# A two-layer graph network in one core: every engine's program reordered, and the row maxima of four heads turned, negated and placed together

## The chip, the cores and the metric

The kernel runs on 1 core of one Trainium2 chip, as one launch. The metric is device time in microseconds. The kernel before was run three times: 1134.08, 1138.78 and 1141.26 us, median 1138.78.

## The reference

16 graphs of 512 nodes with 256 features go through two layers. Everything is float32.

```python
# layer 0, 8 heads of 32, x: (16, 512, 256), adj: (16, 512, 512)
q, k, v = proj(Wq, bq), proj(Wk, bk), proj(Wv, bv)
scores = einsum('bhqd,bhkd->bhqk', q, k) / sqrt(32)
scores = where((adj + eye(n))[:, None] > 0, scores, -inf)
out = einsum('bhqk,bhkd->bhqd', softmax(scores), v) -> (b, n, 256)
h = x + out @ Wo.T + bo
x = (h - mean(h)) * rsqrt(var(h) + 1e-5) * gamma + beta
# layer 1, one head
f = x @ fc_w.T + fc_b
logits = (f @ q_w.T + q_b) + swap(f @ k_w.T + k_b)
masked = leaky_relu(logits + (1 - adj) * -1e9, 0.01)
return softmax(masked) @ f + x
```

## The kernel before, in words

Each engine has a program of its own, written out by hand: `iteration(t)` for t from -1 to 17, and in it 32 steps (`for s in range(POS)`). Iteration t does the attention of graph t, and beside it the first part (turned x, q, k, v, mask) of graph t + 1, the end of layer 0 and the start of layer 1 of graph t - 1, and the end of layer 1 of graph t - 2. `on(t, off)` says whether graph t + off exists. A piece's offset stands in the tables `PE_STEPS`, `ACT_STEPS`, `DVE_STEPS` and `POOL_STEPS`; PE's table also has the step. `Signal.after` turns a piece's name into a semaphore count, so the tables must have the order of the programs.

In every step TensorE (PE) makes one tile of transposed scores for four heads' group g, `st_bank` (a matmul of the stacked halves of q and k, L525, and one that adds the turned mask, L527), and one tile of scores the other way round, `sm_bank` (L535), from which VectorE (DVE) takes the row maxima (L947). ScalarE (ACT) makes the exponentials `e` of the first (L742). The maxima tiles run ahead of the exponentials by `LEAD` = 20 tiles: `maxima_tile(s)` gives tiles 0 to 11 of the next graph at steps 12 to 31, so that group 0 of the next graph begins at step 12 and group 1 at step 28. They read `q_pad`, q of a head among zeros, which four DMAs fill (`pad`, L286); PE waits for them before the first tile of a group.

The row maximum is put into the matmul as a 97th row of `q_stack`. For each head j of 8, PE turns a column of maxima (`turn_max`, L452, [4, 128] out), DVE negates it (`negate_max`, L874) into one of two slots of `neg_max`, and SyncE (SP) places it with a DMA (`place_max`, L291). A slot is written again only once the DMA of two heads before has landed. PE waits for `max_placed[i]` before the first tile of each head.

All DMAs are issued by SP, in one order (`iteration`, L293): adjacency in, `stack(1)` (24 DMAs, L277 and L278, from the halves of q and k into `q_stack` and `k_stack`), `pad(0)` (4), the adjacency again for layer 1, the outputs of graph t - 2, `stack(0)` (24), `pad(1)` (4), x for the residual into `h`, x of graph t + 2, and the eight maxima between them. The wait that opens the iteration on SP is for `l_max3`, DVE's last read of `adj_in` in layer 1.

Everything else on PE goes into three shared PSUM banks in turn (`FILLS`, `bank_of`): a piece waits until the piece three before it in the table has been read (`bank_read`). So the order in `PE_STEPS` also says which reader each piece waits for.

The pieces that the change moves: x turned (`turn_x`), q, k (`project_qk`) and v (`rows_times`); the products with v (`times_v`, L465, `o_bank`); the sums over keys (`total`, L475) of what GpSimd (POOL) added (`add_e`, L1044) and their reciprocals in quarters (DVE, L882); the output projection (`out_project`), residual, statistics and norm (L723); h turned (`turn_h`), `fc_project` and `key_logits`; layer 1's maxima (`layer1_maxima`, L929), leaky relu (`logits`, L677) and exponentials (L684); their turning (`turn_z`, L498) and the product with the features (`attend`, L509), added to h by `finish` (L893). POOL adds `bo` to the residual (L1104).

Of the kernel before, what the change touches and what calls it, by code (L numbers as in the profile page):

```python
# [23 lines left out]
F32R = mybir.dt.float32r  # L24
# [20 lines left out]
LEAD = 20  # L45
# [9 lines left out]
class Signal:  # L55
# [35 lines left out]
    **{f"m{j}": ("dve", f"m{j}") for j in range(NH)}}  # L91
ACT_STEPS = [
# [5 lines left out]
DVE_STEPS = [  # L98
# [5 lines left out]
POOL_STEPS = [  # L104
    ("sum1_3a", -1), ("sum1_3b", -1), ("o_norm0", -1), ("diag", 1), ("sum0_1a", 0), ("o_lo0", -1),
    ("o_norm1", -1), ("o_lo1", -1), ("sum0_1b", 0), ("sum0_2a", 0), ("sum0_2b", 0), ("l_mask", -1), ("sum0_3a", 0),
    ("sum0_3b", 0), ("neg_mean", -1), ("var_eps", -1), ("rstd", -1), ("shift", -1), ("h_gamma", -1), ("h_rest", -1),
    ("sum1_1a", 0), ("sum1_1b", 0), ("x_bo", 0), ("sum1_2a", 0), ("sum1_2b", 0)]
# [8 lines left out]
def build(nc, x, adj, wq, bq, wk, bk, wv, bv, wo, bo, gamma, beta, fc_w, fc_b, q_w, q_b, k_w, k_b, out):  # L117
    with ExitStack() as ctx:
# [47 lines left out]
        neg_max = sb("neg_max", [NT, 2, P], F32R)  # L166
# [55 lines left out]
        max_placed = [Signal(sem(f"max_placed{i}"), [("g1", 0), ("g0", 1)], 16) for i in range(GH)]  # L222
# [23 lines left out]
        def _(sp):  # L246
# [33 lines left out]
            def pad(g, t):  # L280

                sp.wait_ge(act_done.sem, act_done.after(f"q_hi{g}", t))
                sp.wait_ge(sm_done.sem, sm_done.after(27 if g == 0 else 11, t - 1 if g == 0 else t))
# [4 lines left out]
            def place_max(j, t):  # L288
                g, i = j // GH, j % GH
                sp.wait_ge(dve_done.sem, dve_done.after(f"m{j}", t))  # L290
                sp.dma_start(f(q_stack[g][STACK:STACK + 1, i, :]), f(neg_max[:, j % 2, :])).then_inc(max_placed[i].sem, 16)  # L291

            def iteration(t, par):  # L293
# [15 lines left out]
                if on(t, 0):  # L309
                    place_max(6, t)  # L310
                for half in range(2):
                    if on(t, -2):
                        sp.wait_ge(dve_done.sem, dve_done.after(f"fin{half}", t))
                        c = 2 * half
                        sp.dma_start(rows(out, t - 2, c, c + 2), h[par][:, c:c + 2, :]).then_inc(stored[half].sem, 16)
                if on(t, 0):
                    place_max(7, t)
                if on(t, 1):
# [3 lines left out]
                    place_max(0, t)  # L322
# [4 lines left out]
                if on(t, 1):  # L327
                    place_max(1, t)
                    place_max(2, t)
                if on(t, 2):  # L330
                    sp.wait_ge(pool_done.sem, pool_done.after("o_lo1", t))
                    sp.wait_ge(pe_done.sem, pe_done.after("xt1", t))
                    sp.dma_start(x_in[:, :, :], rows(x, t + 2)).then_inc(x_loaded.sem, 16)
                if on(t, 1):
                    place_max(3, t)
# [9 lines left out]
        def _(pe):  # L345
# [28 lines left out]
            def bank_read(name, t):  # L374
# [9 lines left out]
                return made[who].sem, made[who].after(reader, tb)  # L384
# [9 lines left out]
            def iteration(t, par):  # L394
# [52 lines left out]
                def turn_max(j):  # L447

                    pe.wait_ge(max_done.sem, max_done.after((4 * j + 15) % POS, t if j < 4 else t - (1 if 4 * j + 15 < POS else 0)))
                    pe.wait_ge(*bank_read(f"m{j}", t))  # L450
                    bank = bank_of[f"m{j}"]
                    nc.tensor.transpose(bank[0:NT, 0:P], row_max[:, j, :], ident[:, :]).then_inc(pe_done.sem, 1)  # L452
# [61 lines left out]
                for s in range(POS):  # L514
                    g, kt, i = s // (POS // 2), s // GH % NT, s % GH
                    if on(t, 0):
                        if kt == 0 and i == 0:
                            pe.wait_ge(stacked[g].sem, stacked[g].after(f"g{g}", t if g else t - 1))
                            if g == 0:
                                pe.wait_ge(act_done.sem, act_done.after("mt1", t - 1))  # L520
                        if kt == 0:
                            pe.wait_ge(max_placed[i].sem, max_placed[i].after(f"g{g}", t if g else t - 1))
# [14 lines left out]
                    if s == 0:  # L537
                        if on(t, 1):
                            turn_x(0)
                        if on(t, 0):  # L540
                            rows_times("v", 1, xt_hi, xt_lo, WV)
                    if s == 1:
                        if on(t, 1):
                            turn_x(1)
                    if s == 2:
                        if on(t, -1):
                            times_v(0)
                    if s == 3:
                        if on(t, -2):
                            turn_z(0)  # L550
                        if on(t, 0):
                            turn_max(4)
                    if s == 4:
                        if on(t, 1):
                            project_qk("q", WQ, 0)
                    if s == 5:
                        if on(t, -2):
                            turn_z(1)
                        if on(t, -1):
                            total(1)  # L560
                    if s == 6:
                        if on(t, 1):
                            project_qk("k", WK, 0)
                        if on(t, -2):
                            turn_z(2)
                    if s == 7:
                        if on(t, 0):
                            times_v(1)
                            turn_max(5)
                    if s == 8:  # L570
                        if on(t, -2):
                            turn_z(3)
                    if s == 9:
                        if on(t, 0):
                            turn_max(6)
                        if on(t, -2):
                            attend(0)
                    if s == 10:
                        if on(t, 0):
                            times_v(2)  # L580
                        if on(t, -2):
                            attend(1)
                    if s == 11:
                        if on(t, -2):
                            attend(2)
                    if s == 12:
                        if on(t, -2):
                            attend(3)
# [544 lines left out]
```

## Time and profile before

| what | value |
|---|---|
| runs | 1134.08, 1138.78, 1141.26 us |
| profiled execution: time, span | 1139.43 us, 1137.7 us |
| PE busy | 1039.8 us, 91% |
| DVE busy | 741.8 us, 65% |
| POOL busy | 723.9 us, 64% |
| ACT busy | 622.3 us, 55% |
| granted clock of PE, mean | 0.971 |
| chain that ended last | PE 62%, DVE 14%, ACT 11%, issue 6%, POOL 4% |

The busy time of an engine is the union of its instructions. Matmuls are pipelined, and a matmul's duration in the trace (586 ns for L535) is longer than the time after which the next can start, so PE's busy share says less than the distances between starts. The chain of waits shows those distances: it follows the last instruction back, at each step to what released it. The trace repeats from graph 2 on with a period of 65.0 us.

### The profile page before, as it was taken

What the parts mean: (1) busy time and instruction counts of PE and PEld (TensorE: products, weight loads), DVE (VectorE), ACT (ScalarE), POOL (GpSimd) and SP (SyncE); (2) the same over time, 40 slices, a digit from 0 to 9 for tenths busy, and PEclk for the clock granted to TensorE, in tenths of its full rate; (3) what the DMA queues carried; (4) which work ended last, traced back from release to release, by engine and by line L of the source; (5) the groups of instructions that cost most, each with busy time, mean ns of one, the idle gap of its engine ahead of it and who ended that gap; (6) DMA issues with size and microseconds to landing.
All of it is one profiled execution on the core that took longest, in us unless ns stands there. A gap on an engine that the chain in (4) does not pass through costs nothing.

```text
span 1137.7 us, 17894 instructions
## 1 busy us (share of the span) xinstructions
PE 1039.8 (91%) x5896; PEld 653.8 (57%) x5896; DVE 741.8 (65%) x1959; ACT 622.3 (55%) x1178; POOL 723.9 (64%) x415
## 2 busy tenths in 40 slices
PE   4788899999999999999999999999999999999676
PEld 3444455656666565666656565666656566665354
DVE  4554767676766768676766767676676867675332
ACT  2144466574737556564746657473755656474623
POOL 3054686676776666686766667677666668677840
PEclk9798999999999999999999999999999999999967
DMA  5344545353434445353444534353444435334010
GB/s 139 84 103 103 140 103 140 81 134 99 132 101 100 137 104 124 99 135 99 127 113 103 140 83 132 100 133 99 101 137 104 120 102 135 100 80 114 1 56 18
DMA packets 90763, 121.01 MB, mean 106 GB/s; under 512 B 18480, under 2 KB 45616, under 8 KB 90672
## 3 DMA queue, kind: packets, MB, share of 16 engines
q1 hardware_dynamic: 90672, 119.87, 40.4%
q8 instruction: 48, 0.79, 0.3%
q14 instruction: 43, 0.35, 0.1%
HBM read 52.44 MB, written 8.39 MB: 53 GB/s over the span
## 4 chain that ended last, share of the span: by engine, by line
PE 62%; DVE 14%; ACT 11%; issue 6%; POOL 4%; SPq 2%; DMA 1%; ACTq 0%; DVEq 0%; POOLq 0%
PE shared L391 16%; PE shared L509 10%; PE st_bank L525 8%; PE st_bank L527 7%; PE o_bank L465 7%; PE sm_bank L535 7%; DVE recip L882 3%; ACT z L677 3%; DVE sm_bank L947 3%; ACT e L742 3%; POOL e_sum L1044 2%; DVE masks L937 2%; PE shared L498 2%; DVE qt_lo L865 2%; PE shared L484 2%
## 5 line engine op out<-in xcount | busy, mean ns | idle before, releaser
L742 ACT ACTIVATE e<-st_bank 128x512 f32<-128x512 f32 x512 | 309.1, 605 | 396.5 <-PE st_bank L527 394.2
L947 DVE CUSTOM_DVE_ANT_0 sm_bank<-sm_bank,masks 128x512 f32<-128x512 f32 x512 | 351.7, 695 | 239.3 <-PE sm_bank L535 237.4
L535 PE MATMUL sm_bank<-kt_hi,q_pad 128*128 128x512 f32 x512 | 299.0, 586 | 17.0 <-issue 6.0
L1044 POOL TENSOR_TENSOR e_sum<-e_sum,e 128x1024 f32<-128x1024 f32 x128 | 302.2, 2390 | 6.2 <-ACT e L742 5.0
L525 PE MATMUL st_bank<-q_stack,k_stack 97*128 97x512 f32 x512 | 237.1, 464 | 0.8 <-ACT e L742 0.8
L527 PE MATMUL st_bank<-mask_t,ident_b 128*128 128x512 bf16 x512 | 201.7, 394 | 0.0
L1044 POOL TENSOR_TENSOR e_sum<-e 128x1024 f32<-128x1024 f32 x64 | 152.1, 2387 | 10.6 <-PE shared L475 8.2
L525 PEld LDWEIGHTS st_bank<-q_stack,k_stack 97*128 97x128 f32 x512 | 97.4, 190 | 93.6 <-issue 53.7
L465 PE MATMUL o_bank<-e,v 128*32 128x512 f32 x1024 | 137.2, 608 | 1.3 <-ACT e L742 1.3
L509 PE MATMUL shared<-feat,z 128*128 128x256 f32 x512 | 128.3, 397 | 1.4 <-ACT z L689 1.4
L535 PEld LDWEIGHTS sm_bank<-kt_hi,q_pad 128*128 128x128 f32 x512 | 104.7, 205 | 23.2 <-issue 11.9
L509 PEld LDWEIGHTS shared<-feat,z 128*128 128x128 f32 x512 | 98.5, 197 | 31.6 <-issue 11.7
L1096 POOL TENSOR_TENSOR h<-h,gamma_row 128x1024 f32<-128x1024 f32 x16 | 38.3, 2396 | 118.0 <-PE shared L484 118.0
L527 PEld LDWEIGHTS st_bank<-mask_t,ident_b 128*128 128x128 bf16 x512 | 50.1, 98 | 98.7 <-issue 85.5
L391 PE MATMUL shared<-weight_hi,split_hi 128*128 128x256 f32 x256 | 74.6, 292 | 1.5 <-DVE split_lo L861 1.5
L391 PE MATMUL shared<-weight_lo,split_hi 128*128 128x256 f32 x256 | 72.2, 282 | 0.0
L391 PE MATMUL shared<-weight_hi,split_lo 128*128 128x256 f32 x256 | 72.1, 282 | 0.0
L391 PE MATMUL shared<-xt_hi,weight_hi 128*128 128x512 f32 x128 | 52.8, 412 | 20.3 <-DVE qt_lo L865 18.4
L947 DVE DVE_READ_ACCUMULATOR2_ANT row_max<- 128x1 f32 x512 | 71.2, 139 | 0.0
L874 DVE TENSOR_SCALAR neg_max<-shared 4x128 fp32r<-4x128 f32 x128 | 35.0, 274 | 52.1 <-DMA q_stack<-neg_max 47.9
L1049 POOL TENSOR_TENSOR x_in<-x_in 128x512 f32<-128x512 f32 x16 | 20.4, 1274 | 65.0 <-DVE x_in L882 63.3
L882 DVE RECIPROCAL x_in<-x_in 128x128 f32<-128x128 f32 x64 | 55.7, 907 | 9.1 <-ACT x_in L689 9.1
(126 smaller groups left out, 1830.8 us busy)
## 6 DMA issues: line engine op xcount, KB each, us to landing
adj_in<-in_adj SPq DMA_DIRECT2D x32, 1024.0 KB, 5.8
q_stack<-qt_hi SPq DMA_DIRECT2D x256, 64.0 KB, 2.0
k_stack<-kt_hi SPq DMA_DIRECT2D x256, 64.0 KB, 2.0
x_in<-in_x SPq DMA_DIRECT2D x16, 512.0 KB, 4.4
q_pad<-qt_hi SPq DMA_DIRECT2D x128, 64.0 KB, 2.0
q_stack<-qt_lo SPq DMA_DIRECT2D x128, 64.0 KB, 2.0
k_stack<-kt_lo SPq DMA_DIRECT2D x128, 64.0 KB, 2.0
h<-in_x SPq DMA_DIRECT2D x16, 512.0 KB, 3.8
```

What stands on the lines that cost most here:

```text
L391: last = nc.tensor.matmul(bank, a, b, start=(kt == 0 and n == 0), stop=(kt == kts - 1 and n == 2))
L465: last = nc.tensor.matmul(o_bank[i * DH:(i + 1) * DH, :], v[:, kt, o:o + DH], e[:, kt, i, :], start=(kt == 0), stop=(kt == NT - 1))
L509: last = nc.tensor.matmul(bank[:, k * D:(k + 1) * D], z[:, c, kt * P:(kt + 1) * P], feat[:, kt, :], start=(kt == 0), stop=(kt == NT - 1))
L525: nc.tensor.matmul(bank[:, :], k_stack[g][:, i, kt * P:(kt + 1) * P], q_stack[g][:, i, :], start=True, stop=False)
L527: nc.tensor.matmul(bank[:, :], ident_b[:, :], mask_t[par][:, kt, :], start=False, stop=True).then_inc(st_done.sem, 1)
L535: nc.tensor.matmul(sm_bank[s % 2][:, :], q_pad[j // GH][:, j % GH, qt * P:(qt + 1) * P], kt_hi[j // GH][:, :], start=True, stop=True).then ...
L742: nc.scalar.activation(e[:, kt, i, :], st_bank[s % 2][:, :], ACT.Exp, scale=SCALE)\
L874: nc.vector.tensor_scalar(neg_max[:, j % 2, :], bank_of[f"m{j}"][0:NT, 0:P], -1.0, None, ALU.mult)\
L882: last = nc.vector.reciprocal(recip[g][:, n], recip[g][:, n])
L947: nc.vector.tensor_tensor_reduce(sm_bank[s % 2][:, :], sm_bank[s % 2][:, :], mask[nxt if off else par][:, qt * N:(qt + 1) * N], 1.0, LOWES ...
L1044: nc.gpsimd.tensor_tensor(e_sum[:, pair, :], a, b, ALU.add).then_inc(pool_done.sem, 1)
L1096: nc.gpsimd.tensor_tensor(hh[:, :, :], hh[:, :, :], every_row(gamma_row), ALU.mult).then_inc(pool_done.sem, 1)
```

## The change

The eight turned, negated and placed maxima become two, one for each group of four heads: `turn_max(g)` turns [128, 16] at once, `neg_max` has a slot of 16 rows for each group, and one DMA places the 16 rows as 2048 elements of row 97. PE waits for it once, at the first tile of a group. `LEAD` becomes 21, so the groups of the next graph begin at steps 11 and 27. Nearly every other piece has another step. The work itself, apart from the six turns, negations and DMAs fewer, is the same.

```diff
-LEAD = 20
+LEAD = 21
 PE_STEPS = [
-    (0, "xt0", 1), (0, "v1", 0), (1, "xt1", 1), (2, "pv0", -1), (3, "et0", -2), (3, "m4", 0), (4, "q0", 1),
-    (5, "et1", -2), (5, "sum1", -1), (6, "k0", 1), (6, "et2", -2), (7, "pv1", 0), (7, "m5", 0), (8, "et3", -2),
-    (9, "m6", 0), (10, "pv2", 0), (10, "at0", -2), (12, "at1", -2), (13, "op0", -1), (14, "m7", 0),
-    (14, "pv3", 0), (15, "op1", -1), (16, "q1", 1), (17, "mt0", 1), (18, "k1", 1), (18, "m0", 1), (18, "pv4", 0),
-    (21, "sum0", 0), (22, "m1", 1), (22, "pv5", 0), (22, "ht0", -1), (23, "ht1", -1),
-    (25, "mt1", 1), (25, "m2", 1), (26, "pv6", 0), (26, "fc0", -1), (27, "fc1", -1), (28, "kb", -1),
-    (29, "v0", 1), (30, "m3", 1), (30, "pv7", 0)]
+    (0, "pv0", -1), (1, "xt0", 1), (1, "xt1", 1), (4, "sum1", -1), (5, "q0", 1),
+    (6, "k0", 1), (8, "pv1", 0), (8, "et0", -2), (9, "et1", -2), (10, "pv2", 0),
+    (11, "at0", -2), (12, "m1", 0), (12, "et2", -2), (13, "pv3", 0), (14, "et3", -2), (14, "q1", 1),
+    (15, "op0", -1), (16, "op1", -1), (17, "k1", 1), (18, "pv4", 0), (19, "mt0", 1), (20, "sum0", 0), (21, "mt1", 1),
+    (21, "pv5", 0), (22, "ht0", -1), (23, "ht1", -1), (23, "at1", -2), (25, "pv6", 0),
+    (26, "fc0", -1), (27, "fc1", -1), (28, "v0", 1), (28, "m0", 1), (29, "kb", -1), (30, "pv7", 0), (31, "v1", 1)]
 DVE_STEPS = [
...
+    ("x_lo0", 1), ("x_lo1", 1), ("mask", 1), ("q_lo0", 1), ("k_lo0", 1), 
+    ("recip1", -1), ("l_recip", -2), ("m1", 0), ("fin0", -2), ("q_lo1", 1),
+    ("h_add0", -1), ("stats_a", -1), ("h_add1", -1), ("stats_b", -1), ("moments", -1), ("k_lo1", 1), 
+    ("h_lo0", -1), ("h_lo1", -1), ("recip0", 0), ("fin1", -2), ("q_dot0", -1), ("q_dot1", -1), ("m0", 1), ("l_max1", -1),
+    ("l_max3", -1)]
 POOL_STEPS = [
...
+    ("sum1_3a", -1), ("sum1_3b", -1), ("x_bo", -1), ("o_norm0", -1), ("diag", 1), ("sum0_1a", 0), ("o_lo0", -1),
+    ("sum0_1b", 0), ("sum0_2a", 0), ("sum0_2b", 0), ("o_norm1", -1), ("l_mask", -1), ("o_lo1", -1), ("sum0_3a", 0),
+    ("sum0_3b", 0), ("neg_mean", -1), ("var_eps", -1), ("rstd", -1), ("shift", -1), ("sum1_1a", 0), ("sum1_1b", 0),
+    ("h_gamma", -1), ("h_rest", -1), ("sum1_2a", 0), ("sum1_2b", 0)]
-        neg_max = sb("neg_max", [NT, 2, P], F32R)
+        neg_max = sb("neg_max", [GH * NT, NG, P], F32R)
-        max_placed = [Signal(sem(f"max_placed{i}"), [("g1", 0), ("g0", 1)], 16) for i in range(GH)]
+        max_placed = [Signal(sem(f"max_placed{g}"), [("max", 1 - g)], 16) for g in range(NG)]
             # SP
+            def place_max(g, t):
+                sp.wait_ge(dve_done.sem, dve_done.after(f"m{g}", t))
+                sp.dma_start(f(q_stack[g][STACK:STACK + 1, :, :]), f(neg_max[:, g, :])).then_inc(max_placed[g].sem, 16)
             def iteration(t, par):
...
                     stack(1, t)
-                    place_max(4, t)
                 if on(t, 1):
                     pad(0, t)
-                if on(t, 0):
-                    place_max(5, t)
                 if on(t, -1):
...
                     sp.dma_start(adj_in[:, :, :], rows(adj, t - 1)).then_inc(adj_loaded.sem, 16)
+                if on(t, -2):
+                    store(0, t, par)
                 if on(t, 0):
-                    place_max(6, t)
...
+                    place_max(1, t)
                 if on(t, 1):
                     sp.wait_ge(st_done.sem, st_done.after(POS // 2 - 1, t))
                     stack(0, t)
                     pad(1, t)
-                    place_max(0, t)
+                if on(t, 2):
...
+                    sp.dma_start(x_in[:, :, :], rows(x, t + 2)).then_inc(x_loaded.sem, 16)
+                if on(t, -2):
+                    store(1, t, par)
                 if on(t, 0):
...
                     sp.dma_start(h[par][:, :, :], rows(x, t)).then_inc(h_loaded.sem, 16)
                 if on(t, 1):
...
+                    place_max(0, t)
             # PE
-                def turn_max(j):
+                def turn_max(g):
+                    last = (g * GH * NT + GH * NT - 1 - LEAD) % POS
+                    pe.wait_ge(max_done.sem, max_done.after(last, t))
+                    pe.wait_ge(*bank_read(f"m{g}", t))
+                    nc.tensor.transpose(bank_of[f"m{g}"][0:GH * NT, 0:P],
+                                        row_max[:, g * GH:(g + 1) * GH, :].rearrange("p h q -> p (h q)"), ident[:, :])\
+                        .then_inc(pe_done.sem, 1)
                 def attend(c):
...
-                    if c == 0:
-                        pe.wait_ge(act_done.sem, act_done.after("et3", t))
+                    pe.wait_ge(act_done.sem, act_done.after(f"et{c}", t))
             # ACT: logits 2, 3 at steps 0, 1 of the next iteration; exponentials 0 to 3 at steps 4, 6, 8, 10
             # (before: 0, 1, 3, 4); turned_z at 9, 10, 13, 15; turned_mask at 20, 22; o_high(1) at 13
             # DVE: mask halves at steps 4, 5; reciprocals(1) at 8 to 11, reciprocals(0) at 21 to 24;
             # finish at 13 and 25; layer1_maxima at 30 and 31; negate_max(1) at 12, negate_max(0) at 29
```

(The last four lines tell the moved steps of ACT and DVE in words.)

## Rows read from the trace of the kernel before

**Rows 1.** Windows: stretch, its us, busy us of each engine (instructions), PE clock, DMA

```profile
54.52:171.06 116.54, 104.32 (x560) 58.22 (x558) 73.89 (x197) 57.96 (x101) 68.69 (x36) 0.94 0.44 109
171.06:1016.63 845.57, 814.46 (x4759) 513.91 (x4758) 594.67 (x1574) 497.96 (x950) 581.13 (x326) 1.00 0.43 114
1016.63:1137.70 121.07, 90.55 (x457) 59.79 (x455) 46.76 (x120) 54.44 (x110) 64.71 (x39) 0.84 0.17 48
431.25:496.32 65.07, 62.66 (x368) 39.54 (x366) 45.69 (x122) 38.32 (x74) 44.29 (x26) 1.00 0.44 114
...
459.37:496.32 36.95, 36.80 (x226) 23.36 (x224) 24.95 (x76) 20.21 (x36) 27.29 (x16) 1.00 0.37 94
```

**Rows 2.** Chain of waits in the iteration from 431.25: start us, us, what

```profile
457.32 0.24 PE st_bank L525
457.56 0.23 PE st_bank L527
457.79 0.23 PE sm_bank L535
458.02 1.73 PE shared L509 x8
...
462.88 1.40 PE shared L391 x12
...
464.98 0.11 PE shared L452
465.08 1.00 PE o_bank L465 x8
466.08 0.43 PE st_bank L525
...
481.78 0.44 PE shared L484 x4
```

**Rows 3.** Waits over the whole run: engine, line, releaser: total us, times, longest

```profile
PE shared L391 <- DVE qt_lo L865: 18.4, 16, 1.7
...
PE sm_bank L535 <- DMA q_pad<-qt_hi: 4.4, 1, 4.4
```

**Rows 4.** Timeline of DVE: the last instruction of `layer1_maxima`

```profile
431.29 0.08 DVE L929 DVE_READ_ACCUMULATOR2_ANT z<- 128x1 f32 x1
```

**Rows 5.** Timeline of SP's queue from 432.37: first and last of 24 stacks

```profile
432.37 0.59 SPq L291 DMA_DIRECT2D q_stack<-neg_max  x1
433.00 0.44 SPq L296 DMA_DIRECT2D adj_in<-in_adj  x1
433.54 0.56 SPq L277 DMA_DIRECT2D q_stack<-qt_hi  x1
...
448.58 0.59 SPq L278 DMA_DIRECT2D k_stack<-kt_lo  x1
...
449.94 2.42 SPq L286 DMA_DIRECT2D q_pad<-qt_hi  x4
```

**Rows 6.** The tile q_pad, from 431 to 497: its DMAs

```profile
DMA to landing us min/median/max: 1.9/2.0/2.0
```

**Rows 7.** Timeline of PE at step 12 of graph 0

```profile
73.45 0.39 PE L527 MATMUL st_bank<-mask_t,ident_b 128*128 128x512 bf16 x1
77.09 0.47 PE L535 MATMUL sm_bank<-kt_hi,q_pad 128*128 128x512 f32 x1 [3.26 <-issue]
```

**Rows 8.** Windows around that wait, columns as in rows 1

```profile
73.80:77.10 3.30, 0.04 (x2) 0.04 (x1) 0.65 (x3) 0.60 (x1) 2.34 (x1) 1.00 0.35 80
...
78.80:82.20 3.40, 3.40 (x13) 0.89 (x12) 1.08 (x4) 0.56 (x1) 2.30 (x1) 0.50 0.02 5
```

**Rows 9.** Groups by line: shapes, count | busy us, mean ns | idle before, releasers

```profile
L1104 POOL TENSOR_TENSOR h<-h,bo_row 128x1024 f32<-128x1024 f32 x16 | 38.3, 2395 | 10.1 <-DMA h<-in_x 9.6
L723 ACT ACTIVATE h<-h,shift,rstd 128x256 f32<-128x256 f32 x64 | 35.1, 607 | 13.9 <-POOL shift L1092 13.9
L874 DVE TENSOR_SCALAR neg_max<-shared 4x128 fp32r<-4x128 f32 x128 | 35.0, 274 | 52.1 <-DMA q_stack<-neg_max 47.9 <-PE shared L391 3.7 <-PE shared L452 0.4
```

More of the change, by code:

```diff
@@ L282, in pad @@
                 sp.wait_ge(act_done.sem, act_done.after(f"q_hi{g}", t))
-                sp.wait_ge(sm_done.sem, sm_done.after(27 if g == 0 else 11, t - 1 if g == 0 else t))
+                sp.wait_ge(sm_done.sem, sm_done.after((GH * NT - 1 - LEAD) % POS if g == 0 else (POS - 1 - LEAD) % POS, t - 1 if g == 0 else t))
                 for i in range(GH):
@@ L286, in pad, with store @@
                     sp.dma_start(f(q_pad[g][r, i, :]), f(qt_hi[g][r, :])).then_inc(padded[g].sem, 16)
[L288 to L291, printed above, removed]
+            def place_max(g, t):
+                sp.wait_ge(dve_done.sem, dve_done.after(f"m{g}", t))
+                sp.dma_start(f(q_stack[g][STACK:STACK + 1, :, :]), f(neg_max[:, g, :])).then_inc(max_placed[g].sem, 16)
+            def store(half, t, par):
+                sp.wait_ge(dve_done.sem, dve_done.after(f"fin{half}", t))
+                c = 2 * half
+                sp.dma_start(rows(out, t - 2, c, c + 2), h[par][:, c:c + 2, :]).then_inc(stored[half].sem, 16)
             def iteration(t, par):
@@ L383, in bank_read @@
                 who, reader = READ_BY[other]
-                return made[who].sem, made[who].after(reader, tb)
+                later = OFF[other] - made[who].offs[made[who].place[reader]]
+                return made[who].sem, made[who].after(reader, tb + later)
             def three_terms(bank, terms, kts=DT):
@@ L548, in iteration @@
-                    if s == 3:
+                    if s == 0 and on(t, -1):
+                        times_v(0)
+                    if s == 1 and on(t, 1):
+                        turn_x(0)
+                        turn_x(1)
+                    if s == 4 and on(t, -1):
+                        total(1)
+                    if s == 5 and on(t, 1):
+                        project_qk("q", WQ, 0)
+                    if s == 6 and on(t, 1):
+                        project_qk("k", WK, 0)
+                    if s == 8:
+                        if on(t, 0):
+                            times_v(1)
@@ L566, in iteration @@
[L566 to L582, printed above, removed]
@@ L599, in iteration @@
-                    if s == 16:
+                    if s == 10 and on(t, 0):
+                        times_v(2)
+                    if s in (11, 12) and on(t, -2):
+                        attend(s - 11)
+                    if s == 12 and on(t, 0):
+                        turn_max(1)
+                    if s in (12, 14) and on(t, -2):
+                        turn_z(2 if s == 12 else 3)
+                    if s == 13 and on(t, 0):
+                        times_v(3)
+                    if s == 14:
@@ L609, in iteration @@
                         if on(t, 0):
                             times_v(4)
+                    if s == 19 and on(t, 1):
+                        turn_mask(0)
+                    if s == 20 and on(t, 0):
+                        total(0)
                     if s == 21:
-                        if on(t, 0):
-                            total(0)
-                    if s == 22:
                         if on(t, 1):
-                            turn_max(1)
+                            turn_mask(1)
@@ L696, in values @@
                     act.wait_ge(pe_done.sem, pe_done.after("pv6" if half == 0 else "pv0", t))
-                    copy(v[:, 2 * half:2 * half + 2, :], f"v{half}",
-                         bank_of[f"v{half}"][:, :].rearrange("p (k n) -> p k n", k=2))
+                    act.wait_ge(pe_done.sem, pe_done.after(f"v{half}", t if half == 0 else t - 1))
+                    nc.scalar.copy(v[:, 2 * half:2 * half + 2, :], bank_of[f"v{half}"][:, :].rearrange("p (k n) -> p k n", k=2))\
+                        .then_inc(act_done.sem, 1)
                 def turned_mask(half):
@@ L744, in iteration @@
                     if s == 0 and on(t, -2):
-                        exponentials(0)
-                    if s in (1, 2) and on(t, 1):
-                        if s == 1:
-                            act.wait_ge(pe_done.sem, pe_done.after("v1", t))
-                        copy(xt_hi[:, s - 1, :], f"xt{s - 1}", bank_of[f"xt{s - 1}"][:, :])
-                    if s == 1 and on(t, -2):
-                        exponentials(1)
-                    if s == 2 and on(t, 0):
-                        values(1)
@@ L754, in iteration @@
-                    if s == 3 and on(t, -2):
-                        exponentials(2)
-                    if s == 4 and on(t, -2):
-                        turned_z(0)
-                    if s == 4 and on(t, -1):
+                        logits(2)
+                    if s == 1 and on(t, 0):
+                        values(1)
+                    if s == 1 and on(t, -2):
+                        logits(3)
+                        act.wait_ge(act_done.sem, act_done.after("logit3", t))
+                        nc.scalar.mul(l_negmax[:, :], z[:, :, N], -1.0).then_inc(act_done.sem, 1)
@@ L759, in iteration @@
+                    if s == 2 and on(t, 1):
+                        act.wait_ge(pe_done.sem, pe_done.after("v1", t - 1))
+                        copy(xt_hi[:, 0, :], "xt0", bank_of["xt0"][:, :])
+                        copy(xt_hi[:, 1, :], "xt1", bank_of["xt1"][:, :])
+                    if s == 3 and on(t, -1):
                         copy(o_raw[1][:, :], "pv0", o_bank[:, :])
                     if s == 4 and on(t, -2):
-                        exponentials(3)
-                    if s == 5 and on(t, 1):
+                        exponentials(0)
@@ L763, in iteration @@
+                    if s == 5 and on(t, -1):
+                        copy(recip[1][:, :], "sum1", bank_of["sum1"][:, :])
+                    if s == 6 and on(t, 1):
                         qk_high("q", qt_hi, 0, 0)
                     if s == 6 and on(t, -2):
-                        turned_z(1)
-                    if s == 6 and on(t, -1):
-                        copy(recip[1][:, :], "sum1", bank_of["sum1"][:, :])
+                        exponentials(1)
+                    if s == 7 and on(t, 1):
+                        qk_high("k", kt_hi, 1, 0)
@@ L768, in iteration @@
                     if s == 7 and on(t, -1):
                         o_high(0)
-                    if s == 7 and on(t, 1):
-                        qk_high("k", kt_hi, 1, 0)
-                    if s == 7 and on(t, -2):
+                    if s == 8 and on(t, -2):
+                        exponentials(2)
+                    if s == 9 and on(t, -2):
+                        turned_z(0)
+                    if s == 10 and on(t, -2):
+                        turned_z(1)
+                        exponentials(3)
@@ L866, in qk_lo, with negate_max @@
                                                    f(hi[g][:, :]), ALU.add, ALU.subtract).then_inc(done, 1)
[L868 to L874 removed]
+                def negate_max(g):
+                    dve.wait_ge(pe_done.sem, pe_done.after(f"m{g}", t))
+                    dve.wait_ge(max_placed[g].sem, max_placed[g].after("max", t - 1))
+                    nc.vector.tensor_scalar(neg_max[:, g, :], bank_of[f"m{g}"][0:GH * NT, 0:P], -1.0, None, ALU.mult)\
                         .then_inc(done, 1)
@@ L878, in reciprocals @@
                     if quarters[0] == 0:
-                        dve.wait_ge(act_done.sem, act_done.after(f"sum{g}", t if g else t - 1))
+                        dve.wait_ge(act_done.sem, act_done.after(f"sum{g}", t))
                     for k in quarters:
@@ L931, in layer1_maxima, with make_mask @@
                     last.then_inc(done, 1)
-                def make_mask():
-                    dve.wait_ge(adj_loaded.sem, adj_loaded.after("adj", t))
-                    for c in range(2):
-                        to = slice(c * 2 * N, (c + 1) * 2 * N)
-                        last = nc.vector.tensor_scalar(mask[nxt][:, to], adj_in[:, 2 * c:2 * c + 2, :].rearrange("p c n -> p (c n)"),
-                                                       0.0, -BIG, ALU.is_le, ALU.mult)
-                    last.then_inc(done, 1)
+                def make_mask(c):
+                    if c == 0:
+                        dve.wait_ge(adj_loaded.sem, adj_loaded.after("adj", t))
+                    to = slice(c * 2 * N, (c + 1) * 2 * N)
+                    last = nc.vector.tensor_scalar(mask[nxt][:, to], adj_in[:, 2 * c:2 * c + 2, :].rearrange("p c n -> p (c n)"),
+                                                   0.0, -BIG, ALU.is_le, ALU.mult)
+                    if c == 1:
+                        last.then_inc(done, 1)
                 for s in range(POS):
@@ L970, in iteration @@
                         nc.vector.reciprocal(l_recip[:, :], l_sum[:, :]).then_inc(done, 1)
+                    if s in (8, 9, 10, 11) and on(t, -1):
+                        reciprocals(1, (s - 8,))
+                    if s == 12 and on(t, 0):
+                        negate_max(1)
+                    if s == 13 and on(t, -2):
                         dve.wait_ge(pool_done.sem, pool_done.after("h_rest", t - 1))
                         finish(0)
-                    if s == 13 and on(t, -2):
-                        finish(1)
-                    if s == 14 and on(t, -1):
-                        add_residual(0)
-                    if s == 15 and on(t, 0):
-                        negate_max(7)
-                    if s == 15 and on(t, -1):
-                        statistics(0)
-                    if s == 16 and on(t, -1):
-                        add_residual(1)
-                        statistics(1)
+                    if s == 15 and on(t, 1):
+                        qk_lo("q", 1, 0, qt_lo, qt_hi)
+                    if s in (16, 17) and on(t, -1):
+                        add_residual(s - 16)
+                        statistics(s - 16)
+                    if s == 18 and on(t, 1):
+                        qk_lo("k", 1, 1, kt_lo, kt_hi)
                     if s == 17 and on(t, -1):
@@ L1061, in iteration @@
                     add_e(1, 3, 1)
+                    pool.wait_ge(h_loaded.sem, h_loaded.after("x_again", t - 1))
+                    hh = h[nxt]
+                    nc.gpsimd.tensor_tensor(hh[:, :, :], hh[:, :, :], every_row(bo_row), ALU.add).then_inc(pool_done.sem, 1)
                 if on(t, -1):
```

214 lines of the change are left out of this document (59 added, 155 removed), and 15 rows, old and new, of tables (ACT_STEPS, DVE_STEPS).

## The prediction, made before the changed kernel was run

> **What bounds the kernel now.** I read the windows first. From graph 2 to graph 14 the run is 13 equal periods, 845.57 us together, 65.04 each; ahead lie graphs 0 and 1 (116.54 us), behind are graph 15 and the tail (121.07 us) [rows 1]. PE is busy 62.66 us of one period, but that overstates it, since a matmul's record outlasts the distance to the next. So I priced PE by the chain of waits [rows 2]: 0.24 + 0.23 + 0.23 = 0.70 us for a bare step, 1.40 for a projection of 12 passes (q and k have 6 wider ones, the same 1.40), 1.73 for an `attend`, 1.00 for a product with v and another 0.20 because the score matmul behind it takes 0.43 and not 0.23, the same 1.20 for a `total`, 0.44 for four turned blocks, 0.11 for a turned maximum. A period adds up to: 32 steps 22.4; 8 products and 2 totals 12.0; 2 q and 2 k 5.6; v, output and features, two each, and the key logits 9.8; 4 `attend` 6.9; ten groups of turns (two of them masks, taken at the same 0.44) 4.4; 8 maxima 0.9. That is **62.0 us of work in 65.04**; 3.0 us is waiting. The second half has none to speak of: PE is busy 36.80 of the last 36.95 us, steps 12 to 31 [rows 1]. The waiting is in the first twelve steps, which take 65.07 - 36.95 = 28.1 us, and its largest part is q's projection group waiting for DVE: 18.4 us over 16 graphs on PE alone [rows 3].
>
> **Part 1: six turned maxima fewer.** PE saves 6 x 0.11 = 0.66 us a period [rows 2]. DVE saves 6 x 0.27 = 1.6 us, and the 47.9 us in which it stood before `neg_max` for the DMA of two heads earlier [rows 9], 3.0 a period; DVE isn't the bound on average (45.69 of 65.07 [rows 1]), so this pays only through the waits of the first steps. SP saves six issues of 0.63. The negation of 16 rows I take as that of 4, since its free length is the same 128. No row has the landing of the one larger DMA; I take the 2.0 us of the pads [rows 6], with 0 and 4 as ends.
>
> **Part 2: the first steps, unloaded.** Reciprocals of group 0, `attend` and half of layer 1's activations leave steps 0 to 10 or spread over them. Work up to the first maxima tile of the next graph, which is now at step 11: eleven bare steps and 0.47 are 8.2; `times_v` three times, `total` once 4.8; x turned 0.9; q and k 2.8; two z turned 0.9. Together 17.5 us from the iteration's start; before, step 12 came after 28.1. If nothing else waits, a period is 62.0 - 0.66 = 61.4 us.
>
> **Part 3: SP's queue is now late.** This is where I expect the gain to stop. That tile reads `q_pad`, and `pad(0)` stands on SP behind the adjacency load and 24 stacks. Now: last read of `adj_in` ends at 431.37 [rows 4], 0.1 us after the iteration's start; adjacency at 433.00, first stack at 433.54, the pads at 449.94, a maximum between [rows 5]. The distance from first stack to pads without that maximum (0.72) is 15.7. After the change the adjacency load waits for `layer1_maxima` at steps 30 and 31, one step later and behind one more row maximum on DVE (0.61 to 0.7): I estimate its end at 1.0 us after the start (0.1 to 1.3). Then 0.54 to the first stack, 15.7 to the pads, three issues of 0.62, and 2.0 to land [rows 6]: **21.1 us**. PE is there at 17.5. It stands 3.6 us. Before, the pads landed at 18.7 + 1.85 + 2.0 = 22.6 us after the start and PE came at 28.6, so the same queue cost nothing. The trace has this very wait once: at graph 0, where layer 1 has no work and PE ran ahead, it stood from 73.84 to 77.09 [rows 7], 4.4 us by the waits' own account [rows 3].
>
> From that tile to the next start: before, from step 12, 36.95 - 0.46 = 36.5 us. Now added: a step 0.70, three more `attend` 5.19, two turned z 0.88, half of v 1.40; less three maxima 0.33: 44.3. I take off 0.9 for small waits there that go (bounds 0.4 and 1.4), and add 0.6: ACT now does a mask copy and a sum copy among the four norm activations (607 ns each [rows 9]), so the turning of h comes later. **44.0 us**, and the period is 21.1 + 44.0 = 65.1, between 64.1 and 66.2. The loop closes through SP, so a faster or slower first half changes nothing.
>
> **Part 4: the clock.** At graph 0 the 3.26 us of standing came at full clock, and from 78.8 to 82.2 the granted clock was 0.50, which is 1.2 GHz, while PE was busy all 3.40 us [rows 8]. That did 1.7 us of work in 3.4. Where the slow stretch starts within the wait, less is lost. I take 1.2 us a period, ends 0 and 1.7. The Trainium skill (TensorE: Matmul & The Clock Gate, "HAM oscillation") says that a loop in which PE waits for a DMA in every turn pays for the lower clock in every turn. By the row alone the price is certain once, 1.7 us in the run; by the rule it comes 13 times, and the sum is some 15 us higher. The row agrees with the rule for one wait, and none in this trace shows it repeated.
>
> **Part 5: the ends.** Graph 0's wait of rows 7 ends about 2 us earlier, as SP starts the stacks at once; half of v (1.4) moves ahead of graph 0; graph 1 has no `attend` and is held by the same pads, about 54 us. I sum graphs 0 and 1 to 7 us less (3 to 10). In the tail `bo` is added behind the last sum of exponentials and no longer ahead, 2.4 us [rows 9], the adjacency mask (on POOL) comes ahead of the last low half, and `attend` overlaps more: 3 us less (0 to 6).
>
> **The sum.** 13 x (65.1 + 1.2 - 65.04) = +16; -7 - 3: +6 on the profiled execution's own 1139.4 is 1145. That execution lies 0.65 us above the median of 1138.8, so I say **1144 us**. What I cost at nothing: diagonal, statistics and turned masks, which keep their work and sit beside PE's 44 us; if PE didn't have them as cover they'd cost DVE's and ACT's time, at most 1 us a period.
>
> **The rivals.**
> - *The pads aren't what PE waits for* (the queue is ahead by a reason that I miss, or PE's part before is covered). Period 61.4: 13 x -3.6 = -47, with the ends -57: **1082**. For it: the work sum. Against: 24 issues at 0.63 are the steadiest thing in the trace. 12%.
> - *The pads land, but some 2 us earlier* than I have it, or the second half sheds more waits: period 64 without a slow clock, -13 - 10: **1116**. 10%.
> - *As forecast, but the clock stays at 1.00*: 1130. For it: the many short waits of the steady state never lowered it (1.00 over 845.57 us [rows 1]); against it: rows 8. 25%.
> - *The forecast*, 38%.
> - *Slower: the maxima of group 1 come late.* `place_max(1)` is queued on SP behind `store(0)`, which waits for `finish(0)` of step 13. By my count step 13's maximum ends 1.7 us after the step's start, `finish` 0.9 later, the store takes 1.2 of SP, then an issue and 2.0 to land: 5.9. PE needs it at step 16, 6.3 after. Before, each head's own placement lay apart from the others. If it lands more than 0.4 us later, PE stands there, and `max_placed` now holds all four heads. With 1.5 us a period on top of the forecast: **1164**. Only a page has something on the DMA's own cost: the Trainium skill (DMA: Bandwidth & Descriptors, "Anatomy of one DMA") gives about 2.0 us fixed for another issuing path, by which the sum would stay as it is. 15%.
>
> **How the numbers follow.** Two kernels within 1% (1127.4 to 1150.2) are about what can't be told from no change. Faster: all of the first two rivals and a third of the third, 30%. Slower: the last, and the upper part of the forecast's spread (clock 1.7, 44.9 us behind the pads: 1160), 24%. The rest, 46%, within. The range leaves out the first rival and half of the last: 1110 to 1160.
>
> **What would show it.** PE standing 2.5 to 4.5 us in every period just ahead of an `sm_bank` matmul of step 11, released by the DMA into `q_pad`, and no wait for `qt_lo` in steps 5 and 6. Granted clock under 1.00 in the steady state; 0.97 there means a slow stretch in most periods. If the wait is under 1 us, or PE comes to step 11 later than 20 us after the start, part 2 is wrong. If the period is under 63, part 3 is. If PE waits ahead of step 16's `st_bank`, the last rival holds.

## The result, and the profile after

The changed kernel takes **1148.56 us** (median of 4 runs, 1145.00 to 1151.18), the kernel before 1139.69 beside it (4 runs): ratio 1.0081, 95% interval 1.0057 to 1.0105. So 0.8% slower, where 1144 had been forecast.

The windows of the changed kernel, cut at the starts of graphs 0, 2 and 15 as in [rows 1], and two single periods. Columns as there: busy us of PE, PE's weight loads, DVE, ACT, POOL, then PE's clock.

```profile
55.96:166.71 110.75, 100.10 (x546) 55.80 (x547) 74.67 (x185) 57.30 (x102) 71.95 (x38) 0.97 0.45 115
166.71:1032.79 866.08, 824.61 (x4682) 522.55 (x4681) 592.85 (x1496) 501.10 (x950) 580.66 (x326) 0.97 0.42 111
1032.79:1143.20 110.41, 81.92 (x442) 53.74 (x440) 42.42 (x110) 53.87 (x109) 61.08 (x37) 0.94 0.18 52
569.50:633.98 64.48, 61.93 (x362) 39.20 (x361) 45.61 (x116) 38.54 (x74) 44.67 (x26) 1.00 0.43 115
302.13:370.29 68.16, 64.77 (x362) 41.10 (x361) 45.59 (x116) 38.54 (x74) 44.66 (x26) 0.95 0.41 109
```

The 13 periods take 866.08 us, 66.62 each and not 65.04: 20.5 us lost. The ends give back 16: graphs 0 and 1 took 116.54 and take 110.75, graph 15 and the tail took 121.07 and take 110.41. Ahead of graph 0, which starts at 55.96 and not 54.52, 1.4 more are lost. Of two periods one lasts 64.48 us at full clock, less than any of before, the other 68.16 at 0.95. The profiled execution is the fastest of the four, 1145.00 us.

The waits of PE on other things, the counterpart of [rows 3]. The wait for `qt_lo` is no longer among them. Sixteen waits ahead of the maxima tile, `sm_bank`, stand first; 13 of them, 40.3 us, are one in each period, 2.5 to 4.0 us long.

```profile
PE sm_bank L529 <- issue: 47.9, 16, 4.0
...
PE sm_bank L529 <- DMA q_pad<-qt_hi: 5.6, 2, 3.4
```

Three timelines of the period at full clock from 569.50: the last of layer 1's maxima on DVE, SP's adjacency, first and last stack and pads, and PE at step 11.

```profile
570.11 0.08 DVE L881 DVE_READ_ACCUMULATOR2_ANT z<- 128x1 f32 x1
```

```profile
570.22 0.37 SPq L300 DMA_DIRECT2D adj_in<-in_adj  x1
570.69 0.51 SPq L276 DMA_DIRECT2D q_stack<-qt_hi  x1
...
585.18 0.59 SPq L277 DMA_DIRECT2D k_stack<-kt_lo  x1
585.87 2.43 SPq L285 DMA_DIRECT2D q_pad<-qt_hi  x4
588.40 0.53 SPq L309 DMA_DIRECT2D adj_in<-in_adj  x1
```

```profile
586.61 0.49 PE L519 MATMUL st_bank<-q_stack,k_stack 97*128 97x512 f32 x1
586.95 0.39 PE L521 MATMUL st_bank<-mask_t,ident_b 128*128 128x512 bf16 x1
589.81 0.47 PE L529 MATMUL sm_bank<-kt_hi,q_pad 128*128 128x512 f32 x1 [2.48 <-issue]
```

Step 11 starts 17.1 us after the start of the period, and its two score matmuls take PE to about 17.7. The four pads go out from 16.4 to 18.2 and land 2.0 later, at 20.2, and the tile starts at 20.3. The trace names "issue" as what ended the wait, since it doesn't tie these landings to the matmul; the landing is 0.1 us ahead of it in every period. From the tile to the next start it is 44.2 us, in which PE is busy all the time:

```profile
589.80:633.98 44.18, 44.12 (x265) 30.03 (x266) 30.92 (x81) 22.24 (x40) 29.80 (x18) 1.00 0.37 102
```

In the longer period the same wait, 3.32 us, ends in a stretch at 0.50, the lower level of 1.2 GHz. It began 0.9 us before the wait ended, and PE works through the rest of it:

```profile
323.29 0.76 PE L529 MATMUL sm_bank<-kt_hi,q_pad 128*128 128x512 f32 x1 [3.32 <-issue]
```

```profile
323.40:326.80 3.40, 3.40 (x8) 2.71 (x9) 1.56 (x3) 0.00 (x0) 1.50 (x2) 0.50 0.84 288
323.30:370.29 46.99, 46.94 (x265) 31.90 (x266) 30.90 (x81) 22.24 (x40) 28.91 (x18) 0.94 0.36 95
```

From this tile to the next start it is 47.0 us and not 44.2. The 13 periods fall into three kinds. Four are at full clock, 44.1 to 44.2 us behind the tile; five have one stretch of 3.4 us at the lower level, 45.5 to 45.9 behind it; four have 6.8 us of it, 46.7 to 47.0 behind it. Added up, the lower level costs 19 us behind the tiles. The length of the wait alone doesn't decide which kind a period is: behind a wait of 2.49 us the clock was at the lower level (66.14 us, clock 0.97), and behind one of 3.15 it was not (65.13 us, clock 1.00).

```profile
721.81 0.76 PE L529 MATMUL sm_bank<-kt_hi,q_pad 128*128 128x512 f32 x1 [2.49 <-issue]
853.23 0.47 PE L529 MATMUL sm_bank<-kt_hi,q_pad 128*128 128x512 f32 x1 [3.15 <-issue]
```

### The profile page after: what moved, and what is told of

Read it like the earlier page. It is cut to its first block and busy times, and to the rows that moved or that the text cites. A ratio compares the mean times of both kernels' runs of the same rounds, so it can differ in the third digit from the quotient of the medians.

```text
span 1143.2 us, 17238 instructions
## 1 busy us (share of the span) xinstructions
PE 1039.5 (91%) x5800; PEld 656.8 (57%) x5800; DVE 737.4 (65%) x1863; ACT 624.2 (55%) x1178; POOL 723.1 (63%) x415
## 5 line engine op out<-in xcount | busy, mean ns | idle before, releaser
L529 PE MATMUL sm_bank<-kt_hi,q_pad 128*128 128x512 f32 x512 | 299.5, 587 | 57.1 <-issue 47.9
L504 PE MATMUL shared<-feat,z 128*128 128x256 f32 x512 | 137.9, 419 | 2.1 <-ACT z L640 2.1
L504 PEld LDWEIGHTS shared<-feat,z 128*128 128x128 f32 x512 | 108.6, 215 | 20.3 <-ACT z L640 2.7
L1006 POOL TENSOR_SCALAR_AFFINE_SELECT masks<-masks 128x512 bf16<-128x512 bf16 x16 | 10.3, 641 | 121.5 <-DVE masks L889 121.5
L834 DVE RECIPROCAL recip<-recip 128x128 f32<-128x128 f32 x64 | 60.5, 946 | 12.8 <-ACT recip L640 12.7
L834 DVE RECIPROCAL x_in<-x_in 128x128 f32<-128x128 f32 x64 | 60.1, 944 | 4.5 <-ACT x_in L640 4.5
L386 PEld LDWEIGHTS shared<-weight_hi,split_hi 128*128 128x128 f32 x256 | 48.2, 188 | 7.6 <-POOL split_lo L990 5.9
```

The costliest lines, as they stand in the source:

```text
L386: last = nc.tensor.matmul(bank, a, b, start=(kt == 0 and n == 0), stop=(kt == kts - 1 and n == 2))
L504: last = nc.tensor.matmul(bank[:, k * D:(k + 1) * D], z[:, c, kt * P:(kt + 1) * P], feat[:, kt, :], start=(kt == 0), stop=(kt == NT - 1))
L529: nc.tensor.matmul(sm_bank[s % 2][:, :], q_pad[j // GH][:, j % GH, qt * P:(qt + 1) * P], kt_hi[j // GH][:, :], start=True, stop=True).then ...
L834: last = nc.vector.reciprocal(recip[g][:, n], recip[g][:, n])
L1006: nc.gpsimd.affine_select(out=mask_diag[nxt], in_=mask_diag[nxt], compare_op=ALU.not_equal, fill=0.0, base=0, pattern=[[0, NT], [-1, P]], ...
```

## The experiments

The theory: SP's queue of 24 stacks ahead of the pads holds each period from its front, and the wait lets the clock fall behind it. The times below come with the kernel before on the same chip: 1140.19 us in the first four, 1139.10 in the last four.

### 1. The pads earlier

```diff
-                    stack(1, t)
+                    stack(1, t, (0, 1))
                 if on(t, 1):
                     pad(0, t)
+                if on(t, 0):
+                    stack(1, t, (2, 3))
```

> The changed kernel, with the four DMAs into q_pad of group 0 moved on SP between the 12 stacks of two heads and the 12 of the other two. Theory (the pads behind 24 stacks hold the period): they land about 14.6 us after the start of a period, PE comes to the tile of step 11 at 17.1 and doesn't wait there; the next thing late is layer 1's adjacency, still behind all stacks: it lands near 26.7, its mask and the last low half end near 30, and PE stands some 2 to 3 us ahead of the output projection of step 15. Period about 64.5 us, time 1110 to 1130. Rival (the tile waits for something else, such as DVE's row maxima): the wait ahead of step 11 stays and the time is that of the changed kernel, 1148.

Measured: 1125.69 us, ratio 0.9877 (0.9841 to 0.9913). The tile of step 11 no longer waits. PE waits instead ahead of the output projection, for the low half that POOL makes once the adjacency is there. PE's waits, and POOL in the period from 295.77:

```profile
PE shared L388 <- POOL split_lo L992: 42.4, 16, 7.6
```

```profile
317.62 1.27 POOL L988 TENSOR_TENSOR x_in<-x_in 128x512 f32<-128x512 f32 x1
322.50 1.90 POOL L1021 TENSOR_SCALAR adj_in<-adj_in 128x2048 f32<-128x2048 f32 x1 [3.61 <-DMA adj_in<-in_adj]
324.48 1.26 POOL L992 TENSOR_TENSOR split_lo<-x_in,split_hi 128x512 fp32r<-128x512 f32 x1
```

The low half ends at 325.7, 30.0 us after the start, as expected. PE's projection follows at 325.80, behind a gap of 2.15 us. The 13 periods average 65.5 and not 64.5. This wait, 1.8 to 3.4 us in a period, goes with the lower level too: it comes at or just behind the wait in seven periods, and the six at full clock last 63.8 to 64.9. The profiled execution is the slowest of the four, 1131.19 us. Its 13 periods:

```profile
166.35:1018.47 852.12, 818.68 (x4598) 520.22 (x4681) 594.68 (x1496) 501.06 (x950) 579.71 (x326) 0.98 0.42 113
```

### 2. Pads and second adjacency earlier

The same, and `stack(1, t, (2, 3))` stands behind the second adjacency load.

> As the run before, and the second adjacency load also ahead of the last 12 stacks. Theory: neither the tile of step 11 nor the projection of step 15 waits, the period is PE's work, 61.5 to 62.5 us, the clock stays at 1.00, time 1060 to 1085. Rival (the second half hides other waits, which come out once the first is gone, such as the stacks of group 1, now 3 us later, ahead of step 16): period 64 and more, time over 1110.

Measured: **1077.21 us**, ratio 0.9450 (0.9424 to 0.9475); 6% below the changed kernel. SP's order in the period from 468.94, and the windows of all 13 periods:

```profile
477.03 0.60 SPq L277 DMA_DIRECT2D k_stack<-kt_lo  x1
479.93 2.41 SPq L285 DMA_DIRECT2D q_pad<-qt_hi  x4
482.43 0.53 SPq L309 DMA_DIRECT2D adj_in<-in_adj  x1
483.00 1.58 SPq L276 DMA_DIRECT2D q_stack<-qt_hi  x1
```

```profile
160.24:963.60 803.36, 801.92 (x4598) 509.63 (x4681) 593.39 (x1496) 501.07 (x950) 580.39 (x326) 1.00 0.45 120
```

61.80 us a period at full clock, PE busy 801.92 of 803.36. The prediction's sum of PE's work was 61.4. The second half hid nothing large.

### 3. One tile less of lead

```diff
-LEAD = 21
+LEAD = 20
```

> The changed kernel with LEAD = 20 as before, so that the first tile that reads q_pad is at step 12 and not 11; nothing else differs. Theory: the pads land at 21.1 to 21.3 us as now, but PE has 2.4 us more to do ahead of them and comes at 19.6 to 20; it stands 1 to 1.5 us and not 3.5, the clock stays at 1.00, the period is 62 to 62.5 us, time 1080 to 1095. Rival (the stall is not the pads): same time as the changed kernel, 1148, or slower by the tile less ahead.

Measured: 1092.26 us, ratio 0.9582 (0.9557 to 0.9607). One number is worth 56 us. The pads land as before (20.2 to 21.3), and PE has `attend(0)` and a step ahead of them, 2.4 us. The wait is left at 0.1 to 1.1 us, and the clock holds. PE at step 12 of the period from 415.02, and the windows:

```profile
434.87 0.39 PE L521 MATMUL st_bank<-mask_t,ident_b 128*128 128x512 bf16 x1
435.84 0.47 PE L529 MATMUL sm_bank<-kt_hi,q_pad 128*128 128x512 f32 x1 [0.58 <-issue]
```

```profile
164.09:979.22 815.13, 805.38 (x4597) 509.46 (x4681) 592.18 (x1496) 501.11 (x950) 580.23 (x326) 1.00 0.44 118
```

### 4. Work inside the wait

```diff
                             pe.wait_ge(act_done.sem, act_done.after(f"k_hi{j // GH}", t))
+                            if j == 0:
+                                pe.wait_ge(max_done.sem, max_done.after((s - 2) % POS, t if s >= 2 else t - 1))
+                                for _ in range(12):
+                                    nc.tensor.matmul(sm_bank[s % 2][:, :], weight_hi[:, WQ, 0, 0:P],
+                                                     weight_hi[:, WQ, :, :].rearrange("p a b -> p (a b)"), start=True, stop=True)
                             pe.wait_ge(padded...)
```

> The changed kernel, with 12 matmuls of constant weights (512 columns each, into the bank that the tile then overwrites) put ahead of PE's wait for the pads, 2.8 us of work inside a wait of 3.5 us. Their results are not used. Theory of the clock: periods keep the 64.5 us that the changed kernel's periods have when its clock doesn't fall, against 66.6 on average; granted clock 1.00 between 100 and 1030 us, time 1115 to 1130. Rival (the differences between periods have another cause than the clock): the time stays at 1148 or more.

Measured: 1123.43 us, ratio 0.9845 (0.9815 to 0.9876). More work makes the changed kernel 25 us faster. The pads come no earlier, but PE spends the wait working, and no stretch between graph 2 and graph 15 is at the lower level:

```profile
376.94 3.12 PE L530 MATMUL sm_bank<-weight_hi 128*128 128x512 f32 x12
379.89 0.39 PE L534 MATMUL sm_bank<-kt_hi,q_pad 128*128 128x512 f32 x1
```

```profile
165.82:1010.67 844.85, 839.68 (x4748) 537.96 (x4837) 593.23 (x1496) 501.13 (x950) 581.46 (x326) 1.00 0.43 114
```

The first six of these periods last 64.5 to 64.7 us, the others 64.9 to 65.7, as the last of the pads then went out up to 1.2 us later. So the clock's price is 866.08 - 844.85 = 21 us of 13 periods; the 19 us counted in the changed kernel's own trace agree. The late queue itself costs 844.85 - 803.36 = 41 us. That is pads and second adjacency together: with the pads alone early (run 1) the 13 periods give back only 14 us. The second adjacency alone early was not tried.

### 5. The merged maxima alone

The kernel before, with `turn_max(g)`, `negate_max(g)`, `place_max(g)` and `max_placed` of the change at steps 12 and 28:

```diff
-    ... (3, "m4", 0) ... (7, "m5", 0) ... (9, "m6", 0) ... (14, "m7", 0) ... (18, "m0", 1) ... (30, "m3", 1) ...
+    ... (12, "m1", 0), (12, "at1", -2) ... (28, "m0", 1), (28, "kb", -1) ...
```

> The kernel before with one part of the change: the maxima of four heads turned, negated and placed as one, at steps 12 and 28, LEAD 20 and every other piece where it was. Theory: PE saves 0.66 us of turns a period, and the waits of the first steps lose DVE's stops before neg_max (3.0 us a period of DVE, of which PE feels less than 1): period 63.5 to 64.4, time 1118 to 1131. Rival (the turns and negations lie in waits of the first steps and pay nothing): 1135 to 1141. Rival (the one DMA now holds four heads and comes late ahead of step 16 or of the next start): slower than 1145.

Measured: 1121.20 us, ratio 0.9846 (0.9830 to 0.9863). This part of the change is good by itself. How is less plain than expected. The 13 periods give only 3.2 us; the rest comes from the ends: 2.2 ahead of graph 0, 7.9 in graphs 0 and 1 (108.7 us and not 116.5), 5.9 behind. Five periods last 63.9, as expected, eight 65.3 to 65.4. In every period PE waits ahead of k's projection in step 6 until DVE has read q's out of the same bank (`qt_lo`). Before, that wait was 1.1 us and never went with a slower clock. Now PE comes there 0.8 us sooner, since the wait of 0.6 us for `neg_max` ahead of `total` is gone, DVE is no sooner, and the wait is 2.0. It is the same 2.0 us in all thirteen periods, and in eight of them the clock falls:

```profile
PE shared L380 <- DVE qt_lo L846: 31.1, 16, 2.2
```

The wait before, and with the merged maxima:

```profile
445.17 0.47 PE L391 MATMUL shared<-xt_hi,weight_hi 128*128 128x512 f32 x1 [1.12 <-DVE qt_lo L865]
```

```profile
433.54 0.47 PE L380 MATMUL shared<-xt_hi,weight_hi 128*128 128x512 f32 x1 [2.00 <-DVE qt_lo L846]
```

```profile
290.31:355.66 65.35, 63.36 (x356) 40.13 (x360) 45.23 (x116) 38.12 (x74) 44.67 (x26) 0.97 0.42 114
355.66:419.52 63.86, 61.86 (x354) 38.99 (x360) 45.23 (x116) 38.12 (x74) 44.72 (x26) 1.00 0.42 116
```

### 6. The control: pads earlier in the kernel before

The edit of run 1 in the kernel before, its placements of maxima 4 and 5 behind the two halves of the stacks.

> The kernel before, its pads moved between the 12 stacks of two heads and the 12 of the others, as in the run that helped the changed kernel. Theory (before, the pads landed 6 us ahead of need, so SP's queue cost nothing): no difference, 1136 to 1143. Rival (SP's order costs both kernels): faster by more than 1%.

Measured: 1131.71 us, ratio 0.9938 (0.9918 to 0.9959): under the 1136 to 1143 expected and less than the rival's 1%, a miss, by a place that [rows 7] already show. The periods are the same, 845.44 us for 845.57. In graphs 0 and 1 the wait of 3.26 us is gone, and of 14.0 us at the lower level 3.4 are left; together that is 6 us. Another 3.4 us come off the tail (117.6 for 121.1), whose order was not touched; its clock was 0.88 and not 0.84.

```profile
54.34:164.83 110.49, 100.11 (x549) 56.51 (x558) 73.94 (x197) 58.12 (x102) 68.72 (x36) 0.98 0.45 115
164.83:1010.27 845.44, 814.72 (x4677) 514.02 (x4758) 595.30 (x1574) 497.07 (x950) 581.11 (x326) 1.00 0.42 114
```

### 7. Six turns put back

```diff
+                        if s in (3, 7, 10, 18, 22, 26):
+                            nc.tensor.transpose(sm_bank[s % 2][0:NT, 0:P], ident[:, 0:NT], ident[:, :])
```

> The changed kernel with pads and second adjacency early, and six turns of 4 columns of the identity more in a period, each into the bank that the maxima tile behind it overwrites; their results are not used. It gives back PE's part of what merging took away, without negations and DMAs. Theory: where PE is the bound, each costs its 0.11 us: period 61.7 + 0.66 = 62.4, time 1083 to 1089 against 1077. Rival (PE has room between its matmuls): 1077.

Measured: 1085.22 us, ratio 0.9525 (0.9506 to 0.9543), against 1077.21 for run 2 and 1076.62 for run 8, which was on the same chip. The periods take 810.10 and not 803.36 us: 6.7 by 78 turns, 0.09 each.

```profile
159.34:969.44 810.10, 809.08 (x4676) 514.51 (x4759) 593.92 (x1496) 501.13 (x950) 580.02 (x326) 1.00 0.45 119
```

### 8. Both edits

Run 2 with `LEAD = 20`.

> The changed kernel with pads and second adjacency early and LEAD = 20. Theory: with the pads in time the lead of a tile decides nothing, PE's work is the bound: period 61.7 us, time 1074 to 1081. Rival (a lead of 21 is worth something once the stall is gone): slower than 1082.

Measured: 1076.62 us, ratio 0.9452 (0.9436 to 0.9468). The same as run 2: once the pads are in time, the lead decides nothing.

## Why the prediction was right

**Part 1** had PE's price right: 0.11 us a turn said, 0.09 measured where PE is the bound (run 7). As records in the trace the turn of 16 columns takes 280 ns for 275, the negation of 16 rows 276 ns for 274 [rows 9], and DVE's 47.9 us of waiting before `neg_max` for a DMA are gone. The larger DMA landed after 1.9 us, 3.6 at most; 2.0 had been taken.

**Part 2**, PE at the tile of step 11 after 17.5 us: it comes at about 17.7. The waits of the first steps are gone. The largest of them had been read as q's projection; it stood ahead of k's (run 5), which changes no number here.

**Part 3** is the one that decided. First stack at 1.54 said, 1.2 measured, since `layer1_maxima` ends at 0.7 and not 1.0; landing at 21.1 said, 20.2 to 21.8 measured. Behind the tile 44.0 us said, 44.2 measured. The 24 issues, called the steadiest thing in the trace, varied most: 14.5 to 16.0 us from the first start to the last. Runs 1 and 3 show the cause by its place: move the pads, or PE's need of them, and this wait goes or shrinks.

**Part 4**: 1.2 us a period said, 21 us over 13 periods measured (run 4), 1.6 a period; the upper end of 1.7 was passed in four of the periods, which had two slow stretches and lost 2.5 to 2.9. The rule of the Trainium skill (TensorE: Matmul & The Clock Gate, "HAM oscillation") was right to be weighed: the price did come back. It did not come every time, as the rule has it: the lower level came at or behind the same wait in nine of thirteen periods. The prediction read the trace before as showing the price once. That trace has the lower level at or behind four waits ahead of graph 2, of 4.38, 3.26, 2.72 and 1.68 us. This is the stretch behind the last, which ended at 131.79 in graph 1:

```profile
133.40:136.80 3.40, 3.40 (x9) 1.55 (x9) 2.64 (x8) 1.61 (x3) 2.57 (x3) 0.50 0.87 247
```

The 4.4 us that part 3 gives to the wait at graph 0 are the first of these, ahead of graph 0; the one at graph 0 is the 3.26 alone. What decides between the two levels behind waits of 2 to 4 us was not tried.

**Part 5** is the term most off. 7 us less in graphs 0 and 1 said, 5.8 measured, and 1.4 of them only moved: half of v now lies ahead of graph 0, which starts 1.4 us later. Graph 1 was to take about 54 us, held by the pads. It takes 57.3, in run 2 with early pads as well, so the pads don't hold it; PE waits 1.0 us for them there and 2.6 for the low half ahead of the output projection. Behind graph 15 3 us less said (0 to 6), 10.7 measured. The sum had no clock in it there: it rose from 0.84 to 0.94 in this stretch, and PE's busy time fell from 90.55 to 81.92 us. How much of the 10.7 is the clock was not separated; with the maxima merged alone (run 5) the stretch is 5.9 us shorter.

**The sum** came closer than its terms, and that is luck. For the profiled execution +6 was said and +5.6 measured: +20.5 and not +16 in the periods, +1.4 and not 0 ahead of graph 0, -16.5 and not -10 at the ends. The median lies 3.6 us above that execution, at 1148.56; the others ran at a granted clock of 0.957 to 0.960 over the whole run, and it at 0.964. The upper part of the forecast's spread, given as 1160, is 1163 by its own terms.

**The rivals.** The faster one named the right price for the wrong condition: without the late queue the kernel takes 1077 (run 2; 1082 said). "The clock stays" was said at 1130, and is 1123 when made so by run 4. The slower one, maxima of group 1 placed late, has its place but not its price. In the period from 302.13 the DMA goes out at 334.03 and lands 1.9 later, and step 16 starts at 337.70:

```profile
334.03 0.53 SPq L289 DMA_DIRECT2D q_stack<-neg_max  x1
```

```profile
337.70 0.39 PE L519 MATMUL st_bank<-q_stack,k_stack 97*128 97x512 f32 x1
```

That is 1.8 us of slack in nine of the thirteen periods, where 0.4 had been counted, and 1.2 in one; in the other three the landing lay 0.1 to 0.5 us ahead of the step. In run 2 one DMA landed after 4.3 us, at 807.28, and PE stood ahead of step 16: its one period of 62.5 us among those of 61.7 and 61.8. So what that rival describes does happen, but seldom and for 0.5 us; run 8 has it once too, for 0.3.

```profile
807.38 0.47 PE L521 MATMUL st_bank<-q_stack,k_stack 97*128 97x512 f32 x1 [0.53 <-issue]
```

## What to carry to other kernels

When a reordering takes the waits out of one engine, look at who is served by a queue that had slack before: here an adjacency load and 24 DMA issues of 0.63 us stood ahead of a need that came 11 us sooner. Move the urgent few between the many, at the first point where their data exist; that turned 0.8% slower into 5.5% faster. A wait of 2 to 4 us on TensorE can cost another 1.4 to 2.9 through the clock, so work put inside it can pay, even if its result is thrown away.

## What the runs showed of the hardware

From the start of the first to that of the last of 24 DMAs SP took 14.5 us in the best periods of the changed kernel and up to 16.0 in others, because single issues lasted 1.1 to 2.1 us and not 0.59, as one of 1.58 at 483.00 in run 2. Which stretch of the queue that hits differs from period to period; why was not found, and it sets the spread of the changed kernel's periods together with the clock. The second adjacency landed 5.2 to 5.5 us after its issue in the 13 periods of the changed kernel, and 6.1 to 8.0 in those of run 2. The small DMA of the maxima mostly took 1.9 us, but up to 4.3.

In the steady periods waits of PE of up to 1.2 us never went with the lower level (the kernel before, run 3). Waits of 1.8 to 4.0 us did in 24 of 39 periods (the changed kernel 9 of 13, run 1 7 of 13, run 5 8 of 13), and in run 5 the same wait of 2.0 us did in eight periods and not in five.
